# A one-core transformer block: the rows of maxima are issued from ScalarE's queue behind the copy that makes them, not from SyncE's

## The reference

```python
attn = jnp.einsum('bhqd,bhkd->bhqk', Q, K) * scale
attn = jnp.where(causal, attn, -inf)
probs = jax.nn.softmax(attn, axis=-1)
y = jnp.einsum('bhqk,bhkd->bhqd', probs, V)
x = x + y @ W_O.T
```

## Time and profile before

| | |
|---|---|
| median of 3 runs | 901.53 us (901.51 to 903.88) |
| the profiled execution | 900.75 us |
| its span | 899.0 us |
| granted TensorE clock, mean | 0.936 of full |
| busy: PE, DVE, ACT, POOL | 753.9, 526.4, 401.2, 373.2 us |

### The profile page before, as it was taken

The page is one execution under the profiler, slowest core; times in us unless marked ns, Lnnn a source line. Parts: engine busy times, 40 slices in busy tenths (PEclk is TensorE's granted clock), DMA queues, the critical chain, the costliest instruction groups (busy, mean ns, idle before and its releaser), DMA issues. The chain is left out here.

```text
span 899.0 us, 16349 instructions
## 1 busy us (share of the span) xinstructions
PE 753.9 (84%) x5617; PEld 570.8 (63%) x5619; DVE 526.4 (59%) x1154; ACT 401.2 (45%) x777; POOL 373.2 (42%) x670
## 2 busy tenths in 40 slices
PE   2588898989989899898887487999079999799996
PEld 1355565655656556565453466888078999678885
DVE  5366676676766767765660467655035444346666
ACT  3125555455554555555555231444046556432232
POOL 3204455264652636524383225776700000054665
PEclk9779999999999999999988788999679999989998
DMA  5667383663836638266111324677345555445554
GB/s 141 234 240 277 118 296 128 234 213 127 295 120 236 211 137 304 83 231 213 57 58 47 121 78 124 218 261 239 135 148 160 167 163 187 146 141 176 179 176 144
DMA packets 96244, 156.52 MB, mean 174 GB/s; under 512 B 7600, under 2 KB 71088, under 8 KB 91952
## 3 DMA queue, kind: packets, MB, share of 16 engines
q1 hardware_dynamic: 88880, 134.65, 44.6%
q0 software_dynamic: 7296, 20.98, 7.3%
HBM read 85.08 MB, written 70.25 MB: 173 GB/s over the span
## 5 line engine op out<-in xcount | busy, mean ns | idle before, releaser
L609 DVE TENSOR_REDUCE neg_max<-ps_w 128x1 f32<-128x512 f32 (+3 forms) x352 | 200.8, 631 | 67.7 <-PE ps_w L711 67.5
L546 ACT ACTIVATE probs<-ps_w 128x512 f32<-128x512 f32 x320 | 168.2, 611 | 39.4 <-PE ps_w L724 38.0
L408 POOL TENSOR_TENSOR pool_scratch<-minus_half 1x1 f32<-1x1 f32 x190 | 34.8, 183 | 280.4 <-ACT probs L546 203.5
L1066 POOL DMA_INDIRECT srow<-yg_dram,slots x64 | 64.7, 1012 | 175.2 <-DMA yg_dram<-y 133.9
L438 POOL TENSOR_SCALAR_AFFINE_SELECT probs<-probs 128x256 f32<-128x256 f32 (+1 forms) x224 | 93.7, 429 | 0.0
L735 PE MATMUL ps_w<-probs,v_aug 128*32 128x512 f32 (+3 forms) x1024 | 82.5, 466 | 5.8 <-POOL probs L438 5.8
L191 PE MATMUL ps_f<-stacks 128*128 128x512 f32 x176 | 73.9, 420 | 11.4 <-DVE xT_lo_f L1232 8.7
L1052 POOL DMA_INDIRECT xg_dram<-srow,slots x64 | 67.8, 1059 | 30.8 <-issue 17.7
L1083 ACT ACTIVATE silu<-ps_f 128x512 f32<-128x512 f32 (+1 forms) x48 | 28.6, 596 | 111.4 <-PE ps_f L193 111.2
L192 PE MATMUL ps_f<-xT_lo_f,stacks 128*128 128x512 f32 x176 | 71.9, 409 | 0.0
L193 PE MATMUL ps_f<-stacks 128*128 128x512 f32 x176 | 71.8, 408 | 0.0
(11 more groups left out here) (167 smaller groups left out, 1849.7 us busy)
## 6 DMA issues: line engine op xcount, KB each, us to landing
qk_dram<-projected SPq DMA_DIRECT2D x96, 256.0 KB, 4.1
stacks<-qk_dram SPq DMA_DIRECT2D x16, 1024.0 KB, 6.0
xg_dram<-zeros SPq DMA_DIRECT2D x20, 512.0 KB, 10.2
srow<-xg_dram SPq DMA_DIRECT2D x40, 256.0 KB, 2.9
q_st<-qk_dram SPq DMA_DIRECT2D x8, 1024.0 KB, 4.8
k_st<-qk_dram SPq DMA_DIRECT2D x8, 1024.0 KB, 8.1
projected<-experts SPq DMA_DIRECT2D x16, 384.0 KB, 4.7
yg_dram<-projected SPq DMA_DIRECT2D x20, 256.0 KB, 2.2
```

The source lines that it names most:

```text
L408: ticks = Ticks(pool, pool_ticks, lambda: pool.tensor_tensor(out=pool_scratch[:, 0:1], in0=minus_half[0:1, 0:1], in1=minus_half[0:1, 0:1], ...
L546: act.activation(probs[:, g, p * PAIR + half * BANK:p * PAIR + (half + 1) * BANK], ps_w[:, plan.bank(kind, which, half), :], ACT.Exp).then ...
L609: dve.tensor_reduce(out=neg_max[u][:, qt, first:first + len(heads)], in_=bank[:, 0:len(heads) * width].rearrange("p (h n) -> p h n", h=len ...
L1066: pool.indirect_dma_start(out=back[:, m % TB, c, :], out_offset=None, in_=yg_rows, in_offset=bass.IndirectOffsetOnAxis(ap=slots[:, c, n:n ...
```

## The change

`max_rows` of SyncE goes, with its two calls. ScalarE, in step "mT", waits for its own copy and issues the same two DMAs itself. Nothing else is changed: the data, the semaphores that the readers wait for, and the order of the steps stay.

```diff
-        def max_rows(b, u):
-            sp.wait_ge(freed["act"], plan.freed("mT", (b, u))[1])
-            for half in range(HALVES):
-                row = half * ROWS + PART_M
-                sp.dma_start(q_st[u][b % 2][row:row + 1].bitcast(f32).rearrange("o s t -> o (s t)"),
-                             max_row[u][half * SLOTS_U:(half + 1) * SLOTS_U, :].bitcast(f32)).then_inc(max_row_in[u], 16)
-
...
-            if this:
-                max_rows(it, 0)
...
-            if this:
-                max_rows(it, 1)
...
                 act.activation(max_row[u][:, :], bank[0:HU, :], ACT.Copy).then_inc(freed["act"], 1)
+                act.wait_ge(freed["act"], plan.freed("mT", (b, u))[1])
+                for half in range(HALVES):
+                    row = half * ROWS + PART_M
+                    act.dma_start(q_st[u][b % 2][row:row + 1].bitcast(f32).rearrange("o s t -> o (s t)"),
+                                  max_row[u][half * SLOTS_U:(half + 1) * SLOTS_U, :].bitcast(f32)).then_inc(max_row_in[u], 16)
```

## The result

| | before | changed |
|---|---|---|
| median | 902.7 us (901.51 to 903.96, 4 runs) | 948.54 us (941.83 to 955.5, 4 runs) |
| profiled execution, span | 900.75 us, 899.0 us | 948.78 us, 947.1 us |
| mean granted TensorE clock | 0.936 | 0.91 |
| attention (start of the span to the feed-forward part's first TensorE work) | 513.2 us | 559.8 us |
| the rest | 385.8 us | 387.2 us |

The ratio is 1.0508, 95% interval 1.043 to 1.0587. The forecast was 914.2 us, range 905 to 922. The sign was right, the size was not: of the 48.1 us by which the profiled span grew, 46.6 lie in attention.

What follows compares the result with a forecast made beforehand. In-order TensorE was taken as the bound, with ScalarE's x2T copies in unit 1 on its critical path. 10.05 + 3.3 - 0.6 = 12.7 us on the profiled 900.75 gave 913.5, plus 0.8 to the median: 914.2 us, range 905 to 922.

Steps and rivals of the forecast that it cites:

- The sign: Whole kernel: slower by more than 2.7 us, chance 0.87.
- The length of the issue: ScalarE behind each maxima copy: a pair of row DMA issues holds it 1.30 us, as on SyncE.
- Unit 1's wait: Unit 1: x2T copies and L start 1.45 us later in batches 1 to 6, 1.35 in batch 7; together +10.05 us.
- Unit 0's Q copy: Unit 0, batches 1 to 6: ScalarE's Q copy starts 0.55 us later, moving TensorE's L706 equally; +3.3 us.
- The feed-forward part: After attention: as long as before.
- What is removed: SyncE: 32 issues of 0.63 us leave; unit 0's next-batch loads go out some 2 us sooner; worth 0.
- Batch 0's unit 0: Batch 0, unit 0: ScalarE idles 1.97 us before its Q copy, more than the issue takes; loss 0.
- rival C: Unit 0, six batches: rows land with the loads, S 5.15 us later, 941.9 us; half of it 926.6; chance 0.06.
- turns by packets: DMA engines: they alternate between queues packet by packet, so rows are late well inside 0.5 us.
- A term of unknown sign is the clock: TensorE's granted clock: more idle time may move a dip in or out, 1.6 us either way.
- The landing, -0.6 us: Batch 0: on ScalarE's queue rows need not stand behind 1.5 MB of zeros; up to 0.66 us saved, once.
- The forecast's own terms: Attention: +10.05 us in unit 1, +3.3 in unit 0, -0.6 for batch 0's landing; sum 12.7 us.

Runs made afterwards that it cites:

- e7: Kernel before, but ScalarE issues all rows, SyncE's unit 0 loads wait for the rows' landing, x2T steps go ahead of the maxima: 922.21 us beside 926.31, ratio 0.9992.
- e1: Changed kernel, but SyncE waits for unit 0's rows to land before issuing the next batch's loads: 932.74 us, kernel before 907.2, ratio 1.032.
- e3: Kernel before, but ScalarE issues the rows of unit 1 only, SyncE still those of unit 0: 924.7 us, kernel before 907.2, ratio 1.022.
- e12: As e3, with TensorE's waits before L and the maxima's transposes wholly filled by unread matmuls: 925.77 us beside 923.72 before, ratio 1.0046.
- e9: As e3, with six unread matmuls on TensorE partly filling the wait before L: 941.99 us beside 926.31 before, ratio 1.0157.
- e10: Changed kernel, but SyncE waits for ScalarE's copy of unit 0's maxima before issuing the next loads: 951.0 us beside 903.93 before, ratio 1.0531.

## Why the prediction was wrong

The steps that held:

- The length of the issue. 0.58 us on ScalarE, a pair 1.19 to 1.22 in all pairs but the first two (1.81, 1.54), for an assumed 1.30.
- Unit 1's wait. 1.40 us a batch for 1.45; 1.88 in the last (3.28 for 1.40), forecast 1.35. e7 shows the reason is right as well: it is what stands behind the issue.
- Unit 0's Q copy. 0.48 us for 0.55, seen alone in e1; in the changed kernel it disappears in the larger wait.
- The feed-forward part: +1.5 us, forecast unchanged.

The steps that failed, in the order of their size:

1. **"What is removed": the loads that go out 2 us sooner, "Worth 0".** I asked who would read them, and the answer held: in the changed kernel they are first read 41 us after their issue (176.67, 218.18). I did not ask whom they get in front of. They are 2 MB, they keep the DMA engines busy for 6 us, and the rows, awaited 2.95 us after their issue, are what comes next. Waits for rows grew from 4.0 to 23.1 us. SyncE's old wait at the rows had put the transfers in order, and the change took it away. Batch 0's unit 0, which I had put at 0, has such a wait as well (2.58 us). This stood in the prediction as rival C, half of it (2.6 us late, 926.6 us) being very nearly what the rows did; but it had a chance of 0.06 and lay outside the range. The ground for that, 8 KB beside 2 MB and turns by packets, was wrong in its price: beside the loads a row began to move 3.8 to 4.4 us after its issue, not 1.2.
2. **"A term of unknown sign is the clock", 1.6 us either way in all.** The 1.6 us a low stretch costs was read rightly from the earlier trace rows, for unit 1; that longer waits make them come again and again was not seen. Of 48.1 us, 19.1 are waits for rows, 10.3 waits of L (6 x 1.40 and 1.88), 1.5 the feed-forward part, which leaves some 17. The phases tell where these lie: 10.0 in unit 1's phases of batches 1 to 5, 3.3 in unit 0's of batch 0, 3.6 behind the last transposes of the maxima, and only 0.8 in unit 0's phases of batches 1 to 6, which grew by 17.6 us for 16.8 us of waits. For unit 1 the clock is shown as the cause (e3 against e12: 31.4 and 29.7 us a phase). In unit 0 one low stretch of 3.4 us follows the wait in batches 3, 4 and 6 and none in batches 2 and 5; the phases are as long as before plus the wait in the first three, and 0.3 us shorter than that in the other two. So a low stretch cost some 0.35 us there, not 1.6; in batch 1, with 6.8 us of low clock behind the wait, the phase is 1.4 us longer than the wait explains. For the 3.3 and the 3.6 us the clock is only inferred: low stretches lie there, but no kernel filled those waits.
3. **The landing, -0.6 us.** In batch 0, unit 1, S waited 1.38 us in place of 1.63; 0.25 us were gained. A queue of its own brought nothing elsewhere: in batch 7, with free DMA engines, the wait for the rows was 2.35 us (2.37 before).

Either of the first two was enough to leave the range. The forecast's own terms with the clock's answer to them are e1: 3.2% above the kernel before, where 12.7 us had been 1.4% and the range's upper end 2.3%. That includes the late rows in its batch 0, some 3 us. That the change came out slower was forecast for a sound reason, but by a sum that held only a quarter of the loss.

## What to carry to other kernels

A wait on a DMA queue is also an order: before moving a transfer to another queue, look at what was queued behind it, and ask not only who needs those transfers but whose bytes they will now be ahead of. A second queue did not let a small transfer past a large one that had been issued: it moved 3.8 to 4.4 us after its issue here, not 1.2. Hold back the large one until the small one has landed (e1), or keep the two in one queue with the small one first (the kernel before). On an engine that computes, a DMA issue costs its length only to what stands right behind it, so put it in front of a long idle time (e7). And what a new wait of TensorE costs depends on what stands behind it: in unit 1 a wait longer by 1.40 us lengthened the phase by 3.0 us or more, as the clock fell over steps in which TensorE has no gap (5.6 of 5.6 us busy), while in unit 0 16.8 us of waits lengthened the phases by 17.6. Price both before a profile tells.

## What the runs showed of the hardware that was not expected

- The clock's answer to waits: a low stretch behind L in every batch where L waited 2.16 us (e3), none right behind L in batches 1 to 6 where the same time was filled with matmuls nobody reads (e12; one came 10 us later, in one of the five phases of the table), and six of six where it was filled in part (e9).
- Two hardware queues at one set of DMA engines: an 8 KB transfer issued beside 2 MB of loads began to move 3.8 to 4.4 us after the issue, in place of 1.2, whether the loads were issued with it or up to 2.15 us before it. The row pieces ran in the middle of a load, with 51 (changed) and 91 (e10) of its 128 pieces still to start.
- ScalarE's issue is as long as SyncE's, a little less: 0.58 and 0.63 us for the same 8 KB. The loads' issue beside it was no longer than alone (0.34 and 0.43 us in e10, issued at the same instant; 0.34 and 0.44 in the changed kernel), so no wait for a shared generator showed.
